# A second place in PSUM for the logarithm from the ninth unit on, two places for x instead of three

## The chip, the cores and the metric

The kernel runs on one core of one Trainium2 chip. The core has five engines that work side by side and meet only at semaphores: PE (TensorE, matmuls), DVE (VectorE), ACT (ScalarE), POOL (GpSimd) and SP (SyncE, which here issues all transfers). The metric is the time of one execution on the device, in microseconds (us), lower is better; a median of several runs is given.

## What is computed

Four layers one after another on x of shape (2, 96, 48, 48), each `x = x + layer(group_norm(x))`. The change lies in the first layer, in the part that makes the step sizes of a selective scan (four scan directions k, 192 channels, L = 2304 positions, two images):

```python
dlt, b, c = (dbc[:, :, :R], dbc[:, :, R:R + N], dbc[:, :, R + N:])
dlt = jnp.einsum('bkrl,kdr->bkdl', dlt, dt_proj_w) + dt_proj_b[None, :, :, None]
dlt = jax.nn.softplus(dlt)
dA = dlt[..., None] * A_log[None, :, :, None, :]
phi = jnp.exp(-jnp.cumsum(dA, axis=3))
dbx = dlt[..., None] * jnp.swapaxes(b, 2, 3)[:, :, None] * xs[..., None]
h = phi * jnp.cumsum(dbx / (phi + 1e-12), axis=3)
y = jnp.einsum('bkdln,bknl->bkdl', h, c) + Ds[None, :, :, None]
```

Softplus is computed as max(x, 0) + log(1 + exp(-|x|)), and the sum of the logarithm is corrected and capped: with e = exp(-|x|) the kernel forms max(x, 0) + e + min(log(1 + e) - e, 0).

## The kernel before

`program` runs the stages in a row, and a barrier stands between them: `group_norm`, `l0_project`, `l0_steps`, `l0_scan` and so on. The change is in `l0_steps`, which lies between 119 and 288 us of the span; `l0_scan` follows and takes about half of the program.

`l0_steps` works on U = 36 units: 12 pairs of a row tile (3 tiles of 128 rows = channel and image) and a direction (4), each cut in 3 segments of SEG = 768 positions. For each unit i these steps follow one another:

- PE, L431: x = the up-projection, two matmuls (512 and 256 columns, fp32) into a place of two PSUM banks, `base(i)`.
- ACT, L488: e = |x|, then L497: e = exp(-e), in one of NE = 3 buffers.
- DVE, L538: dl = max(x, 0) + e, in one of ND = 4 buffers. It reads x from PSUM and is the last reader of x; its semaphore `s_s` frees the place of x.
- u = -(1 + e), for even units on ACT (L493), for odd units on DVE (L543), in one of NW = 2 buffers.
- ACT, L505: the logarithm log(-u), written to PSUM.
- DVE, L547: ln = (u + 1) + ln, in place in PSUM; then L551: dl = min(ln, 0) + dl, which is the last reader of the logarithm and raises `s_dl`.
- SP, L383: dl is stored to DRAM. POOL, L585: v = XI (or its turned copy XT) times dl, which SP stores too (L387).

PSUM has 8 banks. Before the change x has two places (banks 0-1, 2-3) up to unit 7, and three from unit 8 on (banks 6-7 as well, once the chunks of b and c that used them have been evacuated). The logarithm has one place, banks 4-5, for all units. So x of unit i waits until L538 of unit i-3 has read (i-2 in the first units), and L505 of a unit waits until L551 of the unit before has read (`act.wait_ge(s_dl, i - 1)`).

The order on each engine is written out by hand as a loop over i, and each loop runs one unit ahead of its last steps. ACT in turn i: L488 of unit i, L493 of unit i-1 (if i-1 is even), L497 of unit i, L505 of unit i-1. DVE in turn i: L538 of unit i, L543 of unit i (if odd), L547 and L551 of unit i-1. PE: x of unit i. ACT also evacuates the chunks of b and c (L462, in turns 1 to 6) and casts them to bf16 parts (L472, L479). POOL computes the remainders of these parts (L559, L566, 128x2304 each) and makes the turned copy XT (L571) at units 0, 14 and 26. SP stores all this in an order of its own: behind dl of unit 6 and of unit 11 it issues four large stores (`c_rows`), and behind others the parts (`part_rows`).

Of the kernel before, what the change touches and what calls it, by code (L numbers as in the profile page):

```python
# [18 lines left out]
ACT = mybir.ActivationFunctionType  # L19
# [9 lines left out]
NC = L // CH  # L29
BANK = 512  # L30
SEG = 2 * CH
# [274 lines left out]
def l0_steps(nc, a, ps, XI, Z, d, w_bc, w_dt, w_up, al):  # L306
# [6 lines left out]
    with ExitStack() as ctx:  # L313
        sb, sem = space(nc, ctx, "l0s")
        NE, NW, ND = 3, 2, 4
# [8 lines left out]
        e, u = sb("e", [128, NE, SEG]), sb("u", [128, NW, SEG])  # L324
# [3 lines left out]
        s_x, s_ab, s_e, s_ln, s_u, s_uv, s_q, s_s, s_dl, s_vv = map(sem, "x ab e ln u uv q s dl vv".split())  # L328
# [3 lines left out]
        s_part = [sem(f"part{i}") for i in range(3)]  # L332
        block = ctx.enter_context(nc.Block())

        SLOT3 = 8

        def slot(i):

            return i % 2 if i < SLOT3 else (i - SLOT3 + 2) % 3

        def base(i):
            return (0, 2, 6)[slot(i)] * BANK

        def before(i):

            return max((j for j in range(i) if slot(j) == slot(i)), default=None)

        def place(i):
            g = i // UN
# [1 line left out]

        def by_vector(i):
            return i % 2 == 1

        LN = 4 * BANK

        @block.sync
        def _(sp):
# [42 lines left out]
        @block.tensor  # L401
        def _(pe):
            for c in range(NC):
                for t in range(T):
                    mm = pe.matmul(ps[:, c * BANK:c * BANK + CH], w_dt[:, t, :], XI[:, t, c * CH:(c + 1) * CH],
                                   start=(t == 0), stop=(t == T - 1))
                mm.then_inc(s_dt, 1)

            def bc_chunk(q):
                m, c = divmod(q, NC)  # L410
                if q >= 2:
                    pe.wait_ge(s_bce, q - 1)
                o = (6 + q % 2) * BANK
                for t in range(T):
                    mm = pe.matmul(ps[:, o:o + CH], w_bc[:, m, t, :], XI[:, t, c * CH:(c + 1) * CH],
                                   start=(t == 0), stop=(t == T - 1))
                mm.then_inc(s_bc, 1)

            def x_unit(i):
                g, _, _, c0 = place(i)  # L420
                if before(i) is None:
                    if slot(i) < 2:
                        pe.wait_ge(s_pa, NC)
                        pe.wait_ge(s_pd, NC)
                    else:
                        pe.wait_ge(s_bce, 2 * NC)
                else:
                    pe.wait_ge(s_s, before(i) + 1)
                o = base(i)
                for lo, hi in ((0, BANK), (BANK, SEG)):  # L430
                    mm = pe.matmul(ps[:, o + lo:o + hi], w_up[:, g, :], P[:, c0 + lo:c0 + hi], start=True, stop=True)  # L431
                mm.then_inc(s_x, 1)

            bc_chunk(0)
            bc_chunk(1)
            x_unit(0)
            x_unit(1)
            for i in range(2, U):
                x_unit(i)
                for q in range(2 * (i - 1), 2 * i):  # L440
                    if q < 2 * NC:
                        bc_chunk(q)

        @block.scalar
        def _(act):
            act.preload_act_table_set("natural_log_exp_and_others")
            act.wait_ge(s_in, 16)
            act.wait_ge(s_one, 1)
            for c in range(NC):
                act.wait_ge(s_dt, c + 1)  # L450
                for k in range(2):
                    rows = slice(32 * k, 32 * k + 32)
                    ins = act.activation(scan_order(P, k)[rows, 8 * c:8 * c + 8, :],
                                         ps[rows, c * BANK:c * BANK + CH].rearrange("p (h w) -> p h w", w=W),
                                         ACT.Identity, bias=one[rows, :])
                ins.then_inc(s_pa, 1)

            def evacuate(q):
                m, c = divmod(q, NC)
                act.wait_ge(s_bc, q + 1)  # L460
                for r in range(2):
                    ins = act.copy(scan_order(bc[:, m, :], 2 * m + r)[64 * r:64 * r + 64, 8 * c:8 * c + 8, :],  # L462
                                   ps[64 * r:64 * r + 64, (6 + q % 2) * BANK:(6 + q % 2) * BANK + CH]
                                   .rearrange("p (h w) -> p h w", w=W))
                ins.then_inc(s_bce, 1)

            def cast_hi(m):
                act.wait_ge(s_bce, NC * (m + 1))
                if m:
                    act.wait_ge(s_part[0], 16 * 4)  # L470
                    act.wait_ge(s_rest, 1)
                act.copy(parts[:, 0, :], bc[:, m, :]).then_inc(s_hi, 1)  # L472

            def cast_mid(m):
                act.wait_ge(s_rest, m + 1)
                if m:
                    act.wait_ge(s_part[1], 16 * 4)
                    act.wait_ge(s_lo, 1)
                act.copy(parts[:, 1, :], rest[:, :]).then_inc(s_mid, 1)  # L479

            for i in range(U + 1):
                if i < U:
                    act.wait_ge(s_x, i + 1)
                    if i >= NE:
                        act.wait_ge(s_s, i - NE + 1)
                        if by_vector(i - NE):
                            act.wait_ge(s_uv, (i - NE) // 2 + 1)
                    act.activation(e[:, i % NE, :], ps[:, base(i):base(i) + SEG], ACT.Abs).then_inc(s_ab, 1)  # L488
                if i and not by_vector(i - 1):
                    act.wait_ge(s_e, i)  # L490
                    if i > NW:
                        act.wait_ge(s_q, i - NW)
                    act.activation(u[:, (i - 1) % NW, :], e[:, (i - 1) % NE, :], ACT.Identity, bias=neg_col[:, :],  # L493
                                   scale=-1.0).then_inc(s_u, 1)
                if i < U:
                    act.wait_ge(s_ab, i + 1)
                    act.activation(e[:, i % NE, :], e[:, i % NE, :], ACT.Exp, scale=-1.0).then_inc(s_e, 1)  # L497
                if i:
                    if by_vector(i - 1):
                        act.wait_ge(s_uv, (i - 1) // 2 + 1)  # L500
                    else:
                        act.wait_ge(s_u, (i - 1) // 2 + 1)
                    if i >= 2:
                        act.wait_ge(s_dl, i - 1)
                    act.activation(ps[:, LN:LN + SEG], u[:, (i - 1) % NW, :], ACT.Ln, scale=-1.0).then_inc(s_ln, 1)  # L505
                if i == 0:
                    act.mul(na[:, :, 0:N], al[:, :, :], -1.0).then_inc(s_na, 1)
                    act.mul(na[:, :, N:2 * N], al[:, :, :], -0.5).then_inc(s_na, 1)
                for q in range(2 * (i - 1), 2 * i):
                    if 0 <= q < 2 * NC:  # L510
                        evacuate(q)
                for m in range(2):
                    if i == 3 + 5 * m:
                        cast_hi(m)
                    if i == 6 + 5 * m:
                        cast_mid(m)

        @block.vector
        def _(dve):
            dve.memset(neg_col[:, :], -1.0).then_inc(s_one, 1)  # L520
            dve.wait_ge(s_in, 16)
            for c in range(NC):
# [4 lines left out]
                                            ps[rows, c * BANK:c * BANK + CH].rearrange("p (h w) -> p h w", w=W),  # L527
                                            one[rows, :], None, ALU.add)
                ins.then_inc(s_pd, 1)
            ln = ps[:, LN:LN + SEG]  # L530

            for i in range(U + 1):
                if i < U:
                    dve.wait_ge(s_e, i + 1)
                    if i >= ND:
                        dve.wait_ge(s_vv, i - ND + 1)
                        dve.wait_ge(s_dst[i % ND], 16 * (i // ND))
                    dve.scalar_tensor_tensor(dl[:, i % ND, :], ps[:, base(i):base(i) + SEG], 0.0, e[:, i % NE, :],  # L538
                                             ALU.max, ALU.add).then_inc(s_s, 1)
                    if by_vector(i):  # L540
                        if i >= NW:
                            dve.wait_ge(s_q, i - NW + 1)
                        dve.tensor_scalar(u[:, i % NW, :], e[:, i % NE, :], -1.0, -1.0, ALU.mult, ALU.add  # L543
                                          ).then_inc(s_uv, 1)
                if i:
                    dve.wait_ge(s_ln, i)
                    dve.scalar_tensor_tensor(ln, u[:, (i - 1) % NW, :], 1.0, ln, ALU.add, ALU.add).then_inc(s_q, 1)  # L547
                    dve.wait_ge(s_q, i)
                    dve.wait_ge(s_s, i)
                    ds = dl[:, (i - 1) % ND, :]  # L550
                    dve.scalar_tensor_tensor(ds, ln, 0.0, ds, ALU.min, ALU.add).then_inc(s_dl, 1)  # L551
# [1917 lines left out]
```

## Time and profile before

| | |
|---|---|
| median of 3 runs | 3032.25 us (3024.64 to 3033.62) |
| profiled execution | 3024.85 us, span 3023.0 us |
| granted TensorE clock, mean over the span | 0.921 |
| DVE busy | 2569.6 us (85%) |
| PE, ACT, POOL busy | 2205.4, 1569.5, 1983.6 us |
| the stretch 119 to 292 us: DVE, ACT, POOL, PE busy | 124.67, 120.84, 91.85, 89.83 us of 173 |
| the same stretch: granted clock | 0.81 |
| steps of one unit on DVE: L538, L547, L551 | 0.95, 0.96, 0.96 us each |
| steps of one unit on ACT: L488, L497, L505, L493 | 0.80, 0.84, 0.81, 0.92 us each |

How to read it: the first three lines are times of whole executions. The profile is of one execution, and its rows give start and length of instructions in us from the start of the span. Busy time of an engine is the sum over its instructions; an engine can be idle because it waits for another one, and the profile names that one as the releaser. The granted clock is a share of TensorE's full 2.4 GHz.

### The profile page before, as it was taken

How to read it: one execution, taken by the hardware profiler on the slowest of the kernel's cores; microseconds unless marked ns; L12 is line 12 of the kernel's file. 1: busy time of each engine (PE TensorE's matmuls, PEld its weight loads, DVE VectorE, ACT ScalarE, POOL GpSimd, SP SyncE). 2: the span in 40 equal slices, each digit the busy share in tenths (PEclk: the TensorE clock that was granted, in tenths of full speed). 3: DMA queues.
4: the chain of work that ended last, by engine and by line, in shares of the span. 5: the costliest groups of instructions: out<-in, count | busy, mean ns of one | idle time of the engine just before them, and what ended most of it. 6: DMA issues, size and time to landing. Idle time of an engine off the chain costs nothing. (4 is left out here: it accounts for less than half of the span.)

```text
span 3023.0 us, 25175 instructions
## 1 busy us (share of the span) xinstructions
PE 2205.4 (73%) x7478; PEld 1083.3 (36%) x7478; DVE 2569.6 (85%) x2153; ACT 1569.5 (52%) x2283; POOL 1983.6 (66%) x1119
## 2 busy tenths in 40 slices
PE   6853666767776767777767677778986999688479
PEld 3421223333333333333333333333432555344344
DVE  5677999999999999999999999965887776789630
ACT  2565677677676767767767677743230000362220
POOL 0164999999999999999999999973000000297000
PEclk9977899999999999999999999997997999899689
DMA  1286334333343333334334343343005543100360
GB/s 47 86 240 231 99 104 119 103 121 115 104 123 104 117 114 109 119 102 123 112 110 118 104 118 104 118 142 95 0 0 153 127 112 79 38 8 8 85 86 24
DMA packets 144682, 303.92 MB, mean 101 GB/s; under 512 B 53725, under 2 KB 69220, under 8 KB 139556
## 3 DMA queue, kind: packets, MB, share of 16 engines
q1 hardware_dynamic: 143460, 298.19, 34.2%
q10 hardware_dynamic: 1088, 4.13, 0.6%
q8 instruction: 62, 1.02, 0.1%
q14 instruction: 72, 0.59, 0.1%
HBM read 215.46 MB, written 46.87 MB: 87 GB/s over the span
## 5 line engine op out<-in xcount | busy, mean ns | idle before, releaser
L834 POOL TENSOR_TENSOR l0c_r<-l0c_r,l0c_v 128x768 f32<-128x768 f32 x576 | 1049.2, 1843 | 25.1 <-DVE l0c_r L797 24.4
L864 ACT ACTIVATE ps<-l0c_dlt,l0c_na 128x512 f32<-128x512 f32 (+1 forms) x1152 | 625.9, 575 | 516.6 <-DVE l0c_h L823 502.7
L843 POOL TENSOR_TENSOR l0c_hcp<-l0c_cb,l0c_h 128x768 f32<-128x768 f32 x384 | 707.9, 1844 | 1.5 <-DVE l0c_h L823 1.5
L823 DVE TENSOR_TENSOR_SCAN l0c_h<-ps,l0c_h,l0c_r 128x768 f32<-128x768 f32 x384 | 693.1, 1805 | 1.2 <-issue 1.2
L755 PE MATMUL ps<-l0c_hcp,net_ident 128*128 128x512 f32 (+1 forms) x1536 | 593.4, 511 | 14.0 <-ACT l_Z L857 7.2
L874 ACT ACTIVATE l0c_r<-l0c_S,l0c_floor,l0c_na 128x768 f32<-128x768 f32 x576 | 579.7, 1013 | 0.0
L722 PE MATMUL ps<-l0c_Bp,l0c_sel 96*128 96x512 bf16 (+1 forms) x1152 | 296.7, 340 | 383.5 <-DVE l0c_hcv L804 225.0
L797 DVE SCALAR_TENSOR_TENSOR l0c_r<-l0c_r,ps 128x768 f32<-128x768 f32 x576 | 533.7, 927 | 12.8 <-PE ps L722 7.0
L755 PEld LDWEIGHTS ps<-l0c_hcp,net_ident 128*128 128x128 f32 x1536 | 274.1, 199 | 267.3 <-issue 204.6
L823 DVE TENSOR_TENSOR_SCAN l0c_h<-ps,l0c_r 128x768 f32<-128x768 f32 x192 | 335.2, 1746 | 1.0
L1429 PE MATMUL ps<-l_prod,l_wa 128*96 128x384 f32 (+1 forms) x888 | 292.3, 493 | 26.4 <-DVE l_prod L1390 26.4
L755 PE MATMUL ps<-l0c_hcv,net_ident 128*128 128x512 f32 (+1 forms) x768 | 294.5, 507 | 4.7 <-ACT l_Z L857 2.4
L722 PEld LDWEIGHTS ps<-l0c_Bp,l0c_sel 96*128 96x128 bf16 x1152 | 89.1, 99 | 569.2 <-DVE l0c_r L797 473.6
L1513 POOL MEMSET l2g_pad<- 96x224 f32 x4 | 1.1, 282 | 340.9 <-POOLq L118 340.9
L1429 PEld LDWEIGHTS ps<-l_prod,l_wa 128*96 128x96 f32 (+1 forms) x888 | 146.4, 165 | 171.8 <-issue 161.8
L172 ACT ACTIVATE net_rstd<-gn_t 96x2 f32<-96x2 f32 x4 | 0.8, 203 | 387.1 <-DVE gn_t L143 387.1
L722 PE MATMUL ps<-l0c_Cp,l0c_sel 96*128 96x256 bf16 (+1 forms) x384 | 97.8, 337 | 135.7 <-DVE l0c_r L797 134.6
L755 PEld LDWEIGHTS ps<-l0c_hcv,net_ident 128*128 128x128 f32 x768 | 136.8, 199 | 131.3 <-issue 102.4
L804 DVE TENSOR_TENSOR l0c_hcv<-ps,l0c_h 128x768 f32<-128x768 f32 x192 | 181.9, 948 | 0.0
L1628 PE MATMUL ps<-l_rows,l_diag 128*128 128x384 f32 x450 | 153.3, 503 | 35.6 <-ACT l_diag L1534 19.2
L1390 DVE TENSOR_TENSOR l_prod<-l_turned,l_other 128x2304 f32<-128x2304 f32 (+1 forms) x48 | 122.6, 2557 | 47.4 <-PE ps L1429 46.2
L1522 POOL TENSOR_TENSOR l_accp<-l_accp,l_prod 128x1152 f32<-128x1152 f32 x54 | 142.3, 2637 | 29.7 <-ACT l_prod L1547 22.0
(273 smaller groups left out, 2446.8 us busy)
## 6 DMA issues: line engine op xcount, KB each, us to landing
l0c_cb<-cf SPq DMA_DIRECT2D x768, 192.0 KB, 3.4
l_other<-l_p SPq DMA_DIRECT2D x22, 864.0 KB, 5.8
dlt<-l0s_dl SPq DMA_DIRECT2D x36, 384.0 KB, 2.3
v<-l0s_vv SPq DMA_DIRECT2D x36, 384.0 KB, 2.9
l0c_dlt<-dlt SPq DMA_DIRECT2D x36, 384.0 KB, 3.9
l0c_v<-v SPq DMA_DIRECT2D x36, 384.0 KB, 4.5
l_other<-l_p SPq DMA_DIRECT2D x22, 288.0 KB, 6.7
l0c_Bp<-bc SPq DMA_DIRECT2D x36, 144.0 KB, 4.1
```

The lines of the kernel that those rows point to most:

```text
L722: mm = pe.matmul(ps[:, lo:hi], sel[:, t % 2, n * 128:(n + 1) * 128], rows[:, i, lo - at:hi - at], start=True, stop=True)
L755: mm = pe.matmul(ps[:, lo:hi], ident[:, :], hc[:, lo - PY:hi - PY], start=(n == 0), stop=(n == N - 1))
L797: dve.scalar_tensor_tensor(rj, rj, 1.0, b_all, ALU.add, ALU.mult).then_inc(s_ub, 1)
L804: dve.tensor_tensor(hcv[:, dve_steps(j) % NHV, :], c_all, h[:, j % N, :], ALU.mult).then_inc(s_hv, 1)
L823: dve.tensor_tensor_scan(h[:, n, :], da[j % 2], r[:, j % NR, :], init, ALU.mult, ALU.add).then_inc(s_scan, 1)
L834: pool.tensor_tensor(r[:, j % NR, :], r[:, j % NR, :], v[:, (j // N) % 2, :], ALU.mult).then_inc(s_w, 1)
L843: pool.tensor_tensor(hcp[:, p % NHP, :], cb[:, p % NCB, :], h[:, e % N, :], ALU.mult).then_inc(s_hp, 1)
L864: act.activation(da[e % 2][:, part], dlt[:, i, part], ACT.Exp, scale=na[:, i, n:n + 1]).then_inc(done, 1)
L874: act.activation(r[:, j % NR, :], S[:, i, :], ACT.Tanh, bias=floor[:, :], scale=na[:, i, N + n:N + n + 1]).then_inc(s_tanh, 1)
L1429: mm = pe.matmul(ps[0:C, o:o + CH], wa[0:height, i, :], prod[0:height, n % NPR, c * CH:(c + 1) * CH], start=(i == 0), stop=(i == PT - 1))
L1522: pool.tensor_tensor(accp[:, tl, :], accp[:, tl, :], prod[:, g % NPR, :], ALU.add).then_inc(s_ptap, 1)
L1628: mm = pe.matmul(ps[:, o:o + CH], diag[:, tl, i, :], rows[:, tl, dy + 8 * c:dy + 8 * c + 8, dx:dx + W], start=(i == 0), stop=(i == NPE - 1))
```

## The change

The three places of x become two for all units (banks 0-1 and 2-3), and x of unit i waits for L538 of unit i-2 throughout. The two banks that become free (6-7) are the second place of the logarithm from unit 8 on: `log_slot` gives unit 8 the second place, unit 9 the first, and so on in turn. `before(i)` is now the last unit with the same place of the logarithm, so L505 of unit i waits for L551 of unit i-2 from unit 10 on; that of unit 8 waits until the chunks of b and c have left the banks. No instruction is added or taken away, and the order on each engine is the same; only the PSUM addresses and the waits differ.

```diff
-        SLOT3 = 8
-
-        def slot(i):
-
-            return i % 2 if i < SLOT3 else (i - SLOT3 + 2) % 3
+        SECOND = 8
 
         def base(i):
-            return (0, 2, 6)[slot(i)] * BANK
+            return (0, 2)[i % 2] * BANK
+
+        def log_slot(i):
+
+            return 0 if i < SECOND else (i - SECOND + 1) % 2
+
+        def log(i):
+            o = (4, 6)[log_slot(i)] * BANK
+            return ps[:, o:o + SEG]
 
         def before(i):
 
-            return max((j for j in range(i) if slot(j) == slot(i)), default=None)
+            return max((j for j in range(i) if log_slot(j) == log_slot(i)), default=None)
...
             def x_unit(i):
                 g, _, _, c0 = place(i)
-                if before(i) is None:
-                    if slot(i) < 2:
-                        pe.wait_ge(s_pa, NC)
-                        pe.wait_ge(s_pd, NC)
-                    else:
-                        pe.wait_ge(s_bce, 2 * NC)
+                if i < 2:
+                    pe.wait_ge(s_pa, NC)
+                    pe.wait_ge(s_pd, NC)
                 else:
-                    pe.wait_ge(s_s, before(i) + 1)
+                    pe.wait_ge(s_s, i - 1)
...
-                    if i >= 2:
-                        act.wait_ge(s_dl, i - 1)
-                    act.activation(ps[:, LN:LN + SEG], u[:, (i - 1) % NW, :], ACT.Ln, scale=-1.0).then_inc(s_ln, 1)
+                    if before(i - 1) is not None:
+                        act.wait_ge(s_dl, before(i - 1) + 1)
+                    elif log_slot(i - 1):
+                        act.wait_ge(s_bce, 2 * NC)
+                    act.activation(log(i - 1), u[:, (i - 1) % NW, :], ACT.Ln, scale=-1.0).then_inc(s_ln, 1)
...
                 if i:
+                    ln = log(i - 1)
                     dve.wait_ge(s_ln, i)
                     dve.scalar_tensor_tensor(ln, u[:, (i - 1) % NW, :], 1.0, ln, ALU.add, ALU.add).then_inc(s_q, 1)
```

## Rows read from the trace of the kernel before

**Rows 1.** Waits, 119 to 292 us: who waited for whom, total us, times, longest

```profile
ACT ps L505 <- DVE l0s_dl L551: 34.9, 15, 5.1
DVE l0s_dl L538 <- ACT l0s_e L497: 33.4, 21, 5.8
```

**Rows 2.** Windows, 226 to 254 us: busy us of each engine, clock, DMA share

```profile
226.00:254.00 28.00, 12.46 (x32) 5.42 (x32) 26.10 (x29) 21.49 (x28) 16.16 (x9) 1.00 0.58 232
```

**Rows 3.** Timeline of DVE, units 21 to 24: start us, us, line, operation

```profile
233.24 0.94 DVE L538 SCALAR_TENSOR_TENSOR l0s_dl<-ps,l0s_e 128x768 f32<-128x768 f32 x1
234.27 0.96 DVE L547 SCALAR_TENSOR_TENSOR ps<-l0s_u,ps 128x768 f32<-128x768 f32 x1
235.26 0.96 DVE L551 SCALAR_TENSOR_TENSOR l0s_dl<-ps,l0s_dl 128x768 f32<-128x768 f32 x1
236.55 0.96 DVE L538 SCALAR_TENSOR_TENSOR l0s_dl<-ps,l0s_e 128x768 f32<-128x768 f32 x1 [0.33 <-ACT l0s_e L497]
237.42 1.16 DVE L543 TENSOR_SCALAR l0s_u<-l0s_e 128x768 f32<-128x768 f32 x1
238.50 0.95 DVE L547 SCALAR_TENSOR_TENSOR ps<-l0s_u,ps 128x768 f32<-128x768 f32 x1
239.49 0.96 DVE L551 SCALAR_TENSOR_TENSOR l0s_dl<-ps,l0s_dl 128x768 f32<-128x768 f32 x1
240.36 0.95 DVE L538 SCALAR_TENSOR_TENSOR l0s_dl<-ps,l0s_e 128x768 f32<-128x768 f32 x1
```

**Rows 4.** Timeline of ACT, same pair: logarithm of unit 21, exponential of unit 23

```profile
233.42 0.81 ACT L505 ACTIVATE ps<-l0s_u 128x768 f32<-128x768 f32 x1 [1.72 <-DVE l0s_dl L551]
...
235.69 0.83 ACT L497 ACTIVATE l0s_e<-l0s_e 128x768 f32<-128x768 f32 x1
```

**Rows 5.** Timeline of DVE, unit 12

```profile
191.06 0.96 DVE L538 SCALAR_TENSOR_TENSOR l0s_dl<-ps,l0s_e 128x768 f32<-128x768 f32 x1 [2.51 <-ACT l0s_e L497]
191.93 0.95 DVE L547 SCALAR_TENSOR_TENSOR ps<-l0s_u,ps 128x768 f32<-128x768 f32 x1
```

**Rows 6.** Line 543: duration ns min/median/max, first and last start us

```profile
L543 DVE TENSOR_SCALAR l0s_u<-l0s_e x18: 548/1160/3655, 126.4 to 280.8; 128x768 f32<-128x768 f32 x18
```

**Rows 7.** Timeline of POOL, units 13, 21, and 26 to 27

```profile
204.47 2.13 POOL L585 TENSOR_TENSOR l0s_vv<-l0e_XI,l0s_dl 128x768 f32<-128x768 f32 x1
...
236.35 1.81 POOL L585 TENSOR_TENSOR l0s_vv<-l0s_XT,l0s_dl 128x768 f32<-128x768 f32 x1 [1.09 <-DVE l0s_dl L551]
...
252.29 4.53 POOL L571 COPY l0s_XT<-l0e_XI 128x2304 f32<-128x2304 f32 x1
256.67 3.61 POOL L585 TENSOR_TENSOR l0s_vv<-l0e_XI,l0s_dl 128x768 f32<-128x768 f32 x2
```

**Rows 8.** Timeline of DVE, line 543 of units 15, 27 and 29, line 547 of 28

```profile
202.20 2.73 DVE L543 TENSOR_SCALAR l0s_u<-l0s_e 128x768 f32<-128x768 f32 x1
...
251.66 1.10 DVE L543 TENSOR_SCALAR l0s_u<-l0s_e 128x768 f32<-128x768 f32 x1
...
258.72 1.98 DVE L543 TENSOR_SCALAR l0s_u<-l0s_e 128x768 f32<-128x768 f32 x1
260.62 0.95 DVE L547 SCALAR_TENSOR_TENSOR ps<-l0s_u,ps 128x768 f32<-128x768 f32 x1
```

**Rows 9.** Timeline of DVE, line 538 of unit 16

```profile
212.15 0.96 DVE L538 SCALAR_TENSOR_TENSOR l0s_dl<-ps,l0s_e 128x768 f32<-128x768 f32 x1 [5.35 <-DMA dlt<-l0s_dl]
```

**Rows 10.** Timeline, end of the stage: units 34, 35, and SP's next load

```profile
282.90 0.96 DVE L551 SCALAR_TENSOR_TENSOR l0s_dl<-ps,l0s_dl 128x768 f32<-128x768 f32 x1
...
284.80 0.96 DVE L547 SCALAR_TENSOR_TENSOR ps<-l0s_u,ps 128x768 f32<-128x768 f32 x1 [0.94 <-ACT ps L505]
...
291.83 0.34 SPq L688 DMA_DIRECT2D l0c_sel<-in_sel  x1
```

**Rows 11.** Timeline of PE, x of units 27 and 32

```profile
241.36 1.56 PE L431 MATMUL ps<-l0s_P,l0e_w_up 128*128 128x512 f32 x4 [2.25 <-DVE l0s_dl L538]
...
258.86 2.93 PE L431 MATMUL ps<-l0s_P,l0e_w_up 128*128 128x512 f32 x4 [1.72 <-DVE l0s_dl L538]
```

More of the change, by code:

```diff
@@ L353, in by_vector @@
             return i % 2 == 1
-        LN = 4 * BANK
         @block.sync
@@ L529, in _ @@
                 ins.then_inc(s_pd, 1)
-            ln = ps[:, LN:LN + SEG]
             for i in range(U + 1):
```

## The prediction

> **What bounds the kernel now.** The program is four layers in a row with barriers between the stages, so a stage that ends earlier by t starts everything behind it earlier by t. The change touches only the step sizes, from 119 to 288 us of a 3023 us span. I read the waits of that stretch first [rows 1]. The longest wait that the change can reach is ACT's: the logarithm (L505) waits 34.9 us in 15 waits, because it has one place and L551 of the unit before reads it. The next is DVE's own: L538 waits 33.4 us for the exponential (L497). But that table covers the start of the stage too, where ACT also evacuates bc. In the even part behind it DVE is busy 26.10 of 28.00 us [rows 2], and ACT's idle time costs nothing while DVE has work. So the question is how much DVE idles, and that is read off DVE's own rows.
>
> I call the steps of unit i by letters: X (PE, L431), Abs (L488), Exp (L497), Ln (L505), S (L538), U (L543 on DVE for odd units, L493 on ACT for even ones), Q (L547), D (L551), V (POOL, L585). A pair of units on DVE is S even, Q odd, D odd, S odd, U odd, Q even, D even. [Rows 3] show the pair from S of unit 22 at 233.24 to S of unit 24 at 240.36: 7.12 us. DVE stands still in it at two places only: 0.33 us before S23 (waits for Exp), and between S22 and Q21, whose starts are 1.03 us apart. There Q waits for Ln, which ends at 233.42 + 0.81 = 234.23 [rows 4]. Where Ln is long done the same two starts are 0.87 apart, 191.06 to 191.93 [rows 5]. So 0.33 + 0.16 us per pair can be had at most.
>
> **The 0.33 is not to be had, because U is tied to POOL.** U starts at 237.42 and takes 1.16 us [rows 3], though its shortest is 0.55 [rows 6]. It ends at 238.58. V on POOL runs from 236.35 to 238.16 [rows 7]: U ends 0.42 behind it. The same in a long case: U from 202.20 ends at 204.93 [rows 8], 0.4 behind POOL's instruction, which gave way to V at 204.47 [rows 7]. So U, once POOL is at work, ends 0.42 us after POOL's current instruction, however early U began. V in turn starts 0.13 us after D of the odd unit has ended (235.26 + 0.96 + 0.13 = 236.35). So from D odd (235.26) to Q even (238.50) it is 3.24 us with or without the wait before S odd: taking the 0.33 away makes U 0.33 longer.
>
> **What the change does, part by part.**
> (a) *Ln waits for D of two units before instead of one.* Ln23 waits at present until D22 ends (239.49 + 0.96 = 240.45); then it needs only U23, which ends at 238.58 [rows 3]. So it is done before S24 ends, and Q23 follows S24 by 0.87: gain 1.02 or 1.03 less 0.87, 0.155 us per pair. Pairs that follow one another freely are those whose S even is unit 18, 20 ... 34, nine in all. That of unit 28 is counted under (c), so 8 x 0.155 = 1.24.
> (b) *Before unit 17* other waits end last and take the gains back: long instructions on POOL hold U for up to 3.66 us [rows 6], and S16 waits 5.35 us for the store of dl of unit 12 [rows 9], which stands in SP's queue behind four large stores. One 0.155 (at S10) gets through: by D9, V9, POOL's remainder, U11 and D10 it moves SP's queue from the store of unit 10 on. Bounds 0 and 0.155; I take 0.15, since SP issues without a gap from there to unit 12.
> (c) *Unit 29, beside the turned copy.* POOL runs L571 (from 252.29), then two V in a row (256.67, 3.61 us for both): the first ends at 256.67 + 1.80 = 258.47, the second at 260.28 [rows 7]. U29 starts at 258.72, after the first has ended, and is held by the second until 260.70; Q28 follows at 260.62 [rows 8]. In the changed kernel U29 comes sooner. U27 ends at 252.76 [rows 8], tied to POOL, so not moved against it. Q26 starts 0.08 before U27's end, at 252.68; then by the distances of [rows 3, 5] D26 0.99, S28 0.87, Q27 0.87, D27 0.99, S29 0.87, U29 0.87 later, together 5.46: U29 starts at 258.14, 0.33 before 258.47. It is then held by the first V only, ends at 258.47 + 0.42 = 258.89, and Q28 comes at 258.81 instead of 260.62: 1.81. This needs U to be served ahead of a POOL instruction that stands ready behind the current one. U27 shows that: started at 251.66, it ended at 252.76, though L571 had started at 252.29 and takes 4.53 [rows 7, 8]. Bounds of this term: 0.15 (U misses the gap) and 1.81; I take 1.81, since the distances repeat to 0.02 from pair to pair.
> (d) *The end.* Ln35 waits at present for D34 (starts 282.90), and Q35, which waits for Ln35, starts at 284.80, 1.90 later [rows 10]. Then nothing holds it, and Q35 follows D34 by the 0.88 at which any instruction follows D: gain 1.02.
> (e) *x has two places instead of three.* X of unit i waits for S of i-2 instead of i-3. The ring is: S(i-2) ends, X, Abs, U of the even unit on ACT, Exp, S(i). X takes 1.56 us, or 2.93 at the slower clock [rows 11]. On ACT it is 236.52 - 234.23 = 2.29 us from the end of Ln to the end of Exp [rows 4], which is Abs, U and Exp. With 0.05 for each of three hand-overs the ring takes at most 5.4 us; from the end of S to S two units on there are 6.96 - 0.96 = 6.0. So it costs nothing even at the slow clock, and S odd may slip by another 1.1 us before U would start after V's end. Bounds: nothing, and 4.2 us lost, the whole gain.
> (f) No engine's order of instructions changes. X8 and X9, which now wait for S6 and S7, are wanted by ACT only 3 us after they can be ready. Nothing.
>
> Sum: 1.24 + 0.15 + 1.81 + 1.02 = 4.22 us. The next stage starts with SP's loads at 291.83 [rows 10] and moves as a whole. Profiled execution: 3024.85 - 4.2 = 3020.65. It stands 7.4 us below the median of the three runs (3032.25); all four executions lie near 3024.7 or 3033. Against the median the forecast is 3032.25 - 4.2 = **3028.0 us**.
>
> **Two rules from the notes.** For U's hold the 0.42 us behind POOL's end stands. The Trainium skill, SBUF — State Buffer, section on who interferes with whom, says that VectorE and GpSimd share a pair of ports as an exclusive lock for a whole instruction, and that the loser "fully blocks"; by that, and the trace agrees, removing S's wait gains nothing, while shares of a port would give the second rival below. It does not tell which of two waiting instructions comes next, on which (c) rests. For PE the rows show X at 1.56 and 2.93 us. The Trainium skill, TensorE: Matmul & The Clock Gate, Part 1, says that the clock is halved where PE has lately been little busy, which speaks against waiting longer with X; with every X slow the sum would still be 4.2, by the 5.4 above.
>
> **The rivals.**
> - *U29 misses the gap.* 4.2 - 1.66 = 2.5 us gained: 3029.7. For it: only 0.33 us of room. Chance 0.14.
> - *U and POOL share instead of excluding each other*, so that U ends earlier when it starts earlier: nine times 0.33 more, 4.2 + 3.0 = 7.2: 3025.0. Against it: U ends 0.4 behind POOL whether it began 0.7 us before that or 2.3. Chance 0.04.
> - *The ring of x takes the place of the wait*: PE, ACT and DVE turn in step, and the 0.155 per pair and (c) are lost; 0 to 1 us gained (the end's 1.02), 3032. It decides where X takes over 3.5 us. Chance 0.10.
> - *POOL is served first*: if U27, now earlier by 0.33, lost to L571, U27 would end at about 252.3 + 4.1 + 0.4 = 256.8 instead of 252.76: 4.1 lost and (c) with it, 4.2 - 1.8 - 4.1 = 1.7 us slower than before: 3034.0. It decides where L571 starts (252.29), and there U27 would have stood ready for 1.0 us instead of 0.6, which speaks for U. Chance 0.04.
> - *The change does not do what it says*, because Ln still waits for something that ends as late as D: 3032.2. Against it: U23 ends 1.9 us before D22. Chance 0.04.
>
> **How the numbers follow.** Forecast 0.58, rivals 0.36, and 0.06 for something later in the program that answers to the shift. All these cases lie within 9 us, no more than the fastest and slowest of the runs shown (3024.64 and 3033.62), so those set the range: the lower level 3024.6 - 4.2 = 3020.4, with the shared port 3017.5; the upper 3033.6, with the slow rival 3035.3. So 3018 to 3035. A measurement here can tell 0.3% (9.1 us) from no change. No case of the change reaches that alone; only the two levels of the runs can: faster 0.07, same 0.89, slower 0.04.
>
> **What would show it.** In the profile after: L505's waits for L551 gone from unit 18 on; S even to Q odd 0.87 apart; pairs of 6.97 us; U some 1.5 us long instead of 1.16, still ending 0.42 behind V; U29 of about 0.75 us; no wait of Q35 for Ln; SP's first load of the next stage at about 287.6. I am wrong if U's end moves against V's, if S odd still waits for Exp, or if X comes later than ACT is free.

## The result, and the profile after

The changed kernel takes 3022.82 us (median of 19 runs, 3016.34 to 3026.02); the kernel before, measured beside it, 3027.11 us (median of 19 runs, 3024.16 to 3033.62). The ratio is 0.9982, 95% interval 0.9975 to 0.9989: a gain of 5.4 us, between 3.3 and 7.6. That is a real gain and below the 0.3% from which I had called a change faster. The profiled execution after took 3025.32 us (span 3023.5 us), no less than that of before (3024.85, span 3023.0); what is known of the reason stands under "The changed kernel again".

Here is the timeline of DVE in the changed kernel, for the pair that [rows 3] show before (start us, us, line, operation; L537 is the old L538, L542 the old L543):

```profile
232.58 0.94 DVE L537 SCALAR_TENSOR_TENSOR l0s_dl<-ps,l0s_e 128x768 f32<-128x768 f32 x1
233.45 0.95 DVE L547 SCALAR_TENSOR_TENSOR ps<-l0s_u,ps 128x768 f32<-128x768 f32 x1
234.43 0.96 DVE L551 SCALAR_TENSOR_TENSOR l0s_dl<-ps,l0s_dl 128x768 f32<-128x768 f32 x1
235.31 0.95 DVE L537 SCALAR_TENSOR_TENSOR l0s_dl<-ps,l0s_e 128x768 f32<-128x768 f32 x1
236.17 1.58 DVE L542 TENSOR_SCALAR l0s_u<-l0s_e 128x768 f32<-128x768 f32 x1
237.68 0.95 DVE L547 SCALAR_TENSOR_TENSOR ps<-l0s_u,ps 128x768 f32<-128x768 f32 x1
238.66 0.96 DVE L551 SCALAR_TENSOR_TENSOR l0s_dl<-ps,l0s_dl 128x768 f32<-128x768 f32 x1
239.53 0.95 DVE L537 SCALAR_TENSOR_TENSOR l0s_dl<-ps,l0s_e 128x768 f32<-128x768 f32 x1
```

And POOL and ACT beside it, from their own timelines:

```profile
235.52 1.81 POOL L585 TENSOR_TENSOR l0s_vv<-l0s_XT,l0s_dl 128x768 f32<-128x768 f32 x1 [0.91 <-DVE l0s_dl L551]
```

```profile
233.83 0.80 ACT L506 ACTIVATE ps<-l0s_u 128x768 f32<-128x768 f32 x1
235.18 0.81 ACT L487 ACTIVATE l0s_e<-ps 128x768 f32<-128x768 f32 x1 [0.54 <-PE ps L430]
236.02 0.84 ACT L496 ACTIVATE l0s_e<-l0s_e 128x768 f32<-128x768 f32 x1
237.79 0.81 ACT L506 ACTIVATE ps<-l0s_u 128x768 f32<-128x768 f32 x1 [0.93 <-DVE l0s_u L542]
```

Both of DVE's gaps are gone: no wait before the second L537, and L547 follows L537 by 0.87 us instead of 1.03. The logarithm no longer waits for L551, only for U (L542). But U has grown from 1.16 to 1.58 us. It ends at 237.75, and V on POOL ends at 235.52 + 1.81 = 237.33: 0.42 behind it, as before. From L551 (234.43) to L547 (237.68) it is 3.25 us, where it was 3.24. So the pair takes 6.95 us instead of 7.12, a gain of 0.16 or 0.17, and the removed wait of 0.33 sits inside U.

The pair at unit 29, where [rows 7, 8] show U held until the second V was through. DVE, then POOL:

```profile
256.97 0.82 DVE L542 TENSOR_SCALAR l0s_u<-l0s_e 128x768 f32<-128x768 f32 x1
257.71 0.95 DVE L547 SCALAR_TENSOR_TENSOR ps<-l0s_u,ps 128x768 f32<-128x768 f32 x1
```

```profile
251.13 4.55 POOL L571 COPY l0s_XT<-l0e_XI 128x2304 f32<-128x2304 f32 x1
255.56 3.90 POOL L585 TENSOR_TENSOR l0s_vv<-l0e_XI,l0s_dl 128x768 f32<-128x768 f32 x2
```

The second V alone:

```profile
257.33 2.13 POOL L585 TENSOR_TENSOR l0s_vv<-l0e_XI,l0s_dl 128x768 f32<-128x768 f32 x1
```

U took 0.82 us instead of 1.98 and ended at 257.79, some 0.4 after the first V. The second V, started at 257.33, took 2.13 instead of 1.81, so it was V that waited. And the end of the stage, which [rows 10] show before:

```profile
279.48 0.96 DVE L551 SCALAR_TENSOR_TENSOR l0s_dl<-ps,l0s_dl 128x768 f32<-128x768 f32 x1
280.36 0.95 DVE L547 SCALAR_TENSOR_TENSOR ps<-l0s_u,ps 128x768 f32<-128x768 f32 x1
```

```profile
287.50 0.34 SPq L688 DMA_DIRECT2D l0c_sel<-in_sel  x1
```

The next stage starts at 287.50 instead of 291.83, 4.33 us earlier.

### The profile page after: what moved, and what is told of

Same layout as the page of the kernel before. It is cut to its first block and busy times, and to the rows that moved or that the text cites. A ratio compares the mean times of both kernels' runs of the same rounds, so it can differ in the third digit from the quotient of the medians.

```text
span 3023.5 us, 25175 instructions
## 1 busy us (share of the span) xinstructions
PE 2196.0 (73%) x7478; PEld 1078.5 (36%) x7478; DVE 2569.3 (85%) x2153; ACT 1569.9 (52%) x2283; POOL 1983.1 (66%) x1119
## 3 DMA queue, kind: packets, MB, share of 16 engines
q8 instruction: 62, 1.02, 0.1%
## 5 line engine op out<-in xcount | busy, mean ns | idle before, releaser
L843 POOL TENSOR_TENSOR l0c_hcp<-l0c_cb,l0c_h 128x768 f32<-128x768 f32 x384 | 699.1, 1821 | 0.7 <-DVE l0c_h L823 0.6
```

The costliest lines, as they stand in the source:

```text
L843: pool.tensor_tensor(hcp[:, p % NHP, :], cb[:, p % NCB, :], h[:, e % N, :], ALU.mult).then_inc(s_hp, 1)
```

## The experiments

For all of them I give the time from the start of S of unit 0 to the start of D of unit 35 ("whole stage"), and from the start of S of unit 18 ("from unit 18"), behind DVE's last wait for a store (only in v_and_rows DVE waits for one once more, 0.77 us at unit 20). Both are differences of two starts in one profile. "Pair" is the length that most pairs from unit 18 on have; that of unit 28, beside the turned copy, differs (7.94 before, 6.19 after), and so do a few others in v_after_u, v_and_rows and x_three. The kernels second28, second27, x_twice, x_three and again were run once each (3027.71, 3025.53, 3028.92, 3047.49 and 3023.07 us), so only their profiles are read.

| kernel | whole stage | from unit 18 | pair |
|---|---|---|---|
| before | 163.04 | 66.74 | 7.12 |
| after | 158.73 | 62.60 | 6.95 |
| x2_log1 | 162.88 | 66.75 | 7.12 |
| second28 | 161.38 | 65.01 | 7.12, at the end 6.95 |
| second27 | 160.45 | 63.48 | 7.12, at the end 6.95 |
| v_after_u_one_log | 156.88 | 60.64 | 6.51 |
| v_after_u | 151.42 | 55.38 | 5.93 |
| x_twice | 161.36 | 62.72 | 6.95 |
| x_three | 180.58 | 73.14 | 7.74 |
| v_and_rows | 158.06 | 59.28 | 5.93 |
| again | 158.78 | 62.61 | 6.95 |

### x with two places, the logarithm with one (x2_log1)

```diff
-        SECOND = 8
+        SECOND = U
```

> One part of the change alone: x has two places for all units, the logarithm keeps its one place (SECOND = 36). Measure: from the start of S of unit 0 to the start of D of unit 35, 163.04 us in the profile before and 158.73 in the profile after. Theory (U tied to POOL, the ring of x has room): x costs nothing, 163.0, within 0.2; DVE's pairs stay at 7.12 us. Rival (the ring of x takes part of the gain): 0.2 to 0.4 us more per pair, 165 to 167.

162.88 us, and 66.75 from unit 18 on where before has 66.74. Against before the ratio is 0.9999 (0.9989 to 1.0008). The third place of x was worth nothing, so its loss costs nothing, and all of the gain is the logarithm's.

### The second place from unit 28, and from unit 27 (second28, second27)

```diff
-        SECOND = 8
+        SECOND = 28
```

> The second place of the logarithm from unit 28 on instead of unit 8, x with two places. Ln of unit 27 still waits for D of unit 26, so S of unit 29 still waits 0.33 and U of unit 29 starts after the first of the two V has ended. Theory: three S-to-Q gains of 0.155 (units 30, 32, 34) and 1.02 at the end, 163.04 - 1.49 = 161.55 from S of unit 0 to D of unit 35; U of unit 29 is 1.98 us long. Rival (U simply gets shorter or longer with DVE's own order, POOL has no part): as with the second place from 27 on, within 0.2.

> The second place of the logarithm from unit 27 on, one unit earlier than in the run with 28. Now Ln of unit 27 waits for nothing of DVE but U, S of unit 29 is not held, and U of unit 29 starts about 0.23 us before the first V ends. Theory (U waits for POOL's current instruction only): U of unit 29 takes about 0.65 us instead of 1.98, and the stage is 1.81 shorter than with 28: 159.74. Rival (no lock, or POOL's next instruction comes first): 0.16 to 0.5 us shorter than with 28, 161.1 to 161.4.

These two differ by one unit in a number, and their U of unit 29 does not start at the same point against V. In second28 (DVE, then POOL):

```profile
256.41 0.96 DVE L537 SCALAR_TENSOR_TENSOR l0s_dl<-ps,l0s_e 128x768 f32<-128x768 f32 x1 [0.33 <-ACT l0s_e L496]
257.29 1.95 DVE L542 TENSOR_SCALAR l0s_u<-l0s_e 128x768 f32<-128x768 f32 x1
```

```profile
255.23 3.58 POOL L585 TENSOR_TENSOR l0s_vv<-l0e_XI,l0s_dl 128x768 f32<-128x768 f32 x2
```

In second27:

```profile
257.77 0.95 DVE L537 SCALAR_TENSOR_TENSOR l0s_dl<-ps,l0s_e 128x768 f32<-128x768 f32 x1
258.64 0.84 DVE L542 TENSOR_SCALAR l0s_u<-l0s_e 128x768 f32<-128x768 f32 x1
```

```profile
257.25 3.91 POOL L585 TENSOR_TENSOR l0s_vv<-l0e_XI,l0s_dl 128x768 f32<-128x768 f32 x2
```

U starts 2.06 us after the first V in the one and 1.39 after it in the other. A V takes 1.8, so the one falls into the second V and takes 1.95, the other into the first and takes 0.84. (I had expected 0.65 for it, from a start 0.23 us before the first V ends; it was 0.41.) From unit 18 on, 65.01 against 63.48. The forecast was 66.74 - 1.49 = 65.25 and 1.81 less, 63.44. The 0.24 by which second28 is shorter than forecast is for the most part its pair of unit 18, which took 6.90 instead of 7.06: L537 of unit 18 had waited 0.44 us for a store, and Ln was done by then. Over the whole stage, on which I had put my expectation (159.74 for second27), the two differ by only 0.93 instead of 1.81. Up to S of unit 16, which waits for a store, second27 took 90.06 us and second28 88.94; the part from unit 18 on is the one that tells.

### V after U, with both places and with one (v_after_u, v_after_u_one_log)

One more wait on POOL, in the changed kernel and in the kernel before:

```diff
                 pool.wait_ge(s_dl, i + 1)
+                if i % 2 and 17 <= i < U - 2:
+                    pool.wait_ge(s_uv, (i + 3) // 2)
```

> The changed kernel with one more wait on POOL: V of an odd unit i from 17 on waits until U of unit i+2 is done, so that DVE's U never stands behind V. Theory (U is tied to V by the shared ports): U of units 19 and on takes 0.55 us instead of 1.5 to 1.58, D odd to Q even falls from 3.24 to 2.23, a pair from 6.95 to 5.96; nine pairs, less the 1.66 already had at unit 29 and up to 1 lost around the turned copy: 151.2 (150 to 153) instead of 158.73 from S of unit 0 to D of unit 35, and the whole time 7 to 8 us less than after. Rival (ACT or the ring of x bounds the pair as well): no more than 0.3 per pair, 156 or more; if V comes too late for the stores, it is slower than after.

> The kernel before (one place for the logarithm, three for x) with the wait of V of odd units from 17 on for U of unit i+2. Theory (two causes in series: POOL's hold of U covers ACT's wait; once the hold is gone, the logarithm's one place bounds): U of 0.55 us, but S odd still waits for Exp, which follows Ln, which waits for D: from D even to the next S odd but one it stays at 4.17 us, then 0.87 + 0.47 + 0.98, so pairs of 6.49 us instead of 7.12; from S of unit 0 to D of unit 35 157 (155.5 to 158.5) against 163.04 before and 151.4 with both. So the second place would be worth 0.5 per pair where U is free, and 0.155 where it is not. Rival (the second place is worth the same either way): pairs of 6.1, 154.

DVE in v_after_u:

```profile
229.54 0.96 DVE L551 SCALAR_TENSOR_TENSOR l0s_dl<-ps,l0s_dl 128x768 f32<-128x768 f32 x1
230.41 0.95 DVE L537 SCALAR_TENSOR_TENSOR l0s_dl<-ps,l0s_e 128x768 f32<-128x768 f32 x1
231.28 0.95 DVE L547 SCALAR_TENSOR_TENSOR ps<-l0s_u,ps 128x768 f32<-128x768 f32 x1
232.27 0.96 DVE L551 SCALAR_TENSOR_TENSOR l0s_dl<-ps,l0s_dl 128x768 f32<-128x768 f32 x1
233.14 0.95 DVE L537 SCALAR_TENSOR_TENSOR l0s_dl<-ps,l0s_e 128x768 f32<-128x768 f32 x1
234.01 0.55 DVE L542 TENSOR_SCALAR l0s_u<-l0s_e 128x768 f32<-128x768 f32 x1
234.47 0.96 DVE L547 SCALAR_TENSOR_TENSOR ps<-l0s_u,ps 128x768 f32<-128x768 f32 x1
```

From L551 at 232.27 to L547 at 234.47 it is 2.20 us instead of 3.24, and U takes 0.55. POOL waits now instead:

```profile
234.79 1.81 POOL L587 TENSOR_TENSOR l0s_vv<-l0s_XT,l0s_dl 128x768 f32<-128x768 f32 x1 [2.32 <-DVE l0s_u L542]
```

The pair is 5.93 us, the stage 151.42 (forecast 151.2). Two pairs are longer: that of unit 28 takes 6.53, since U of unit 29 still stands behind the turned copy (1.17 us), and that of unit 32 takes 6.37. Timed, v_after_u is at 0.9967 of before (0.9955 to 0.9980), 10.0 us, where after is at 0.9982. That is the lowest ratio of this study, and 4.6 us below after. I had expected 7 to 8; the two intervals are too wide to tell these apart. With one place for the logarithm U is as short, but S odd waits for Exp again (v_after_u_one_log):

```profile
234.63 0.96 DVE L538 SCALAR_TENSOR_TENSOR l0s_dl<-ps,l0s_e 128x768 f32<-128x768 f32 x1 [0.33 <-ACT l0s_e L497]
235.50 0.55 DVE L543 TENSOR_SCALAR l0s_u<-l0s_e 128x768 f32<-128x768 f32 x1
235.97 0.96 DVE L547 SCALAR_TENSOR_TENSOR ps<-l0s_u,ps 128x768 f32<-128x768 f32 x1
```

Pairs of 6.51 (forecast 6.49), stage 156.88 (forecast 157), ratio 0.9984 (0.9975 to 0.9993). So the second place of the logarithm is worth 0.17 per pair as long as POOL holds U, and 6.51 - 5.93 = 0.58 once it does not. The two costs lie over one another.

### x computed twice and three times (x_twice, x_three)

```diff
-                for lo, hi in ((0, BANK), (BANK, SEG)):
+                for lo, hi in ((0, BANK), (BANK, SEG)) * 2:
```

> The changed kernel with the two matmuls of x issued twice into the same place, so X takes about 3.1 us at the full clock. Theory (ring of x at most 5.6 of the 6.0 us there are; PE delays X odd by some 0.4 more, and S odd may slip by 1.1 before U is late): 158.7 to 159.2 from S of unit 0 to D of unit 35, as after (158.73); perhaps a wait of S odd for Exp of 0.1 to 0.4 that U swallows. Rival (x is in the ring already): 0.5 to 1.5 us more per pair, 165 or more.

> The changed kernel with the matmuls of x issued three times: X takes about 4.7 us at the full clock. Theory: two X need 9.4 us of PE per pair of 6.95, so PE bounds each pair, at about 9.5 us, in step with S; from S of unit 16 on 9 pairs x 2.5 us more, and much of the units before: 185 or more from S of unit 0 to D of unit 35. This shows what the ring costs when it does decide. Rival: none in earnest; it gives the scale for the run with two.

In x_three the factor is 3. PE in x_twice, two x in a row in 5.57 us, then in x_three (the row begins at the edge of the view):

```profile
230.94 5.57 PE L430 MATMUL ps<-l0s_P,l0e_w_up 128*128 128x512 f32 x16 [0.82 <-DVE l0s_dl L537]
237.90 5.57 PE L430 MATMUL ps<-l0s_P,l0e_w_up 128*128 128x512 f32 x16 [1.38 <-DVE l0s_dl L537]
```

```profile
225.66 20.68 PE L430 MATMUL ps<-l0s_P,l0e_w_up 128*128 128x512 f32 x56
```

With x twice, from unit 18 on the stage takes 62.72 us against 62.60: the ring of x has the room that was claimed. My expectation for the whole stage (158.7 to 159.2) was missed, with 161.36: 2.4 us are lost before unit 16, 1.8 of them by unit 3, where PE has the chunks of b and c to do as well; I had not counted them. With x three times PE does not pause from 224.65 to 274.29 us, and the pair is 7.74 us (180.58 for the stage, where I had expected 185 or more). I had expected pairs of 9.5, from 4.7 us for a tripled x, and that was wrong: one x alone takes 1.56 us for its four matmuls, 0.39 each, while matmuls in a row come every 20.68 / 56 = 0.37 us at mixed clocks and 5.57 / 16 = 0.35 in x_twice. A pair has 24 of them, 7.74 / 24 = 0.32 each. There it is PE's own work that fills the pair, so x_three does not show what the wait for one of two places costs. Up to 5.6 us of PE time per pair the two places cost nothing from unit 18 on; the kernel has about 3.

### The large stores one by one (v_and_rows)

v_after_u, with the stores of the rows of c spread over four units each:

```diff
-            def c_rows(m):
+            def c_rows(m, which):
...
-                for r in range(4):
+                for r in which:
...
-                    if i == 6 + 5 * m:
-                        c_rows(m)
+                    if 0 <= i - 6 - 5 * m < 4:
+                        c_rows(m, [i - 6 - 5 * m])
```

> The changed kernel with V of odd units from 17 on after U of unit i+2, and the four large stores of the rows of c given one per unit (after dl of units 6 to 9 and 11 to 14) instead of four at once. Theory (S of units 11 and 16 wait for stores of dl that stand behind four large stores in SP's queue): these waits, 3.1 and 4.9 us with V moved alone, shrink to 0 to 2 us each, and the stage is 3 to 6 us shorter than with V moved alone: 146 to 148.5 instead of 151.42 from S of unit 0 to D of unit 35. Rival (the transfers themselves are the limit, the queue order is not): the waits move to other units and the stage stays within 1.5 us of 151.4.

Of the waits the rival was right: they moved. L537 of unit 11 no longer waits for a store (2.81 us in v_after_u), but that of unit 12 then waits 7.26 us for Exp instead of 2.89 and starts only 0.1 us earlier. L537 of unit 16 waits 0.72 us instead of 4.9, but those of units 17 and 18 wait 3.57 and 4.25, and that of unit 19 waits 2.96 for Exp:

```profile
207.69 0.96 DVE L537 SCALAR_TENSOR_TENSOR l0s_dl<-ps,l0s_e 128x768 f32<-128x768 f32 x1 [0.72 <-DMA dlt<-l0s_dl]
...
214.07 0.96 DVE L537 SCALAR_TENSOR_TENSOR l0s_dl<-ps,l0s_e 128x768 f32<-128x768 f32 x1 [3.57 <-DMA dlt<-l0s_dl]
...
221.62 0.96 DVE L537 SCALAR_TENSOR_TENSOR l0s_dl<-ps,l0s_e 128x768 f32<-128x768 f32 x1 [4.25 <-DMA dlt<-l0s_dl]
```

The stage is 158.06 us, 6.6 longer than v_after_u, and the ratio to before 0.9984 (0.9975 to 0.9993). So both numbers were missed, the theory's and the rival's 1.5 us. The waits moved and grew. The order in SP's queue does matter, by 6.6 us here, but spreading the large stores loses time; why the waits grew, and whether another order would gain, no run shows.

### The changed kernel again (again)

> The changed kernel once more, unaltered, for one more profile. In the profile after, the stage ends 4.3 us earlier but the span is 0.5 us longer than before: 3.5 us of that come between the end of the scan and the first channel-mixing stage, 1985 to 2130 us. Theory (that part differs from one execution to the next): the stage is again 158.7 from S of unit 0 to D of unit 35, within 0.3, while the time from the start of the next stage to the end of the program is not that of the profile after, but 1 to 5 us away from it. Rival (the shift by 4.3 us is given back there by the change itself): the time behind the stage repeats within 0.5 us.

The stage repeated: 158.78 us. The part behind it did not settle the question as I had put it: it was 2.5 us shorter than in the profile after, yet about as much was lost again before the channel mixing. Its first matmul (L1100) starts at 2100.94 us in before, at 2100.08 in after and at 2100.46 in again, so that of the 4.33 and 4.09 us by which the next stage's first load came earlier only 0.86 and 0.48 are left. Most of what is lost is PE's clock. Here is PE in before and in after, at the start of the same 36 matmuls (L974):

```profile
2056.71 11.77 PE L974 MATMUL ps<-l0n_sq,l0n_avgv 128*2 128x384 f32 x36 [2.89 <-ACT l0n_sq L990]
```

```profile
2052.90 14.71 PE L974 MATMUL ps<-l0n_sq,l0n_avgv 128*2 128x384 f32 x36 [2.89 <-ACT l0n_sq L990]
```

Both follow a pause of PE of 2.89 us. The windows of before and after there (window, us, busy us of PE, PEld, DVE, ACT, POOL, granted clock, DMA share, GB/s):

```profile
2056.90:2059.90 3.00, 3.00 (x10) 0.76 (x9) 0.55 (x1) 0.00 (x0) 2.60 (x3) 1.00 0.79 211
```

```profile
2053.10:2056.10 3.00, 3.00 (x6) 0.56 (x5) 0.00 (x0) 0.00 (x0) 2.46 (x3) 0.50 0.77 232
```

In before the clock stays at 2.4 GHz (1.00); in after it is 1.2 GHz (0.50) for about 6 us, and the matmuls take 2.9 us longer (14.71 against 11.77). Of the eleven profiles of this study, three show the loss there (after, again, second28, each with 14.71 us) and eight do not (11.77 each), v_after_u, second27 and v_after_u_one_log among them, whose stages are shortened too. So neither a shorter stage nor the second place of the logarithm is enough to bring it about. But the changed kernel shows it in both its profiles, and the kernel before was profiled once. If the loss belonged to the changed kernel, 4.3 - 2.9 = 1.4 us would be left of the gain, and the interval of the timed gain (3.3 to 7.6 us) speaks against that. What puts an execution on one side or the other stays open.

The clock is not all of it. From the next stage's first load to the end of the span it is 2731.2 us in before, the shortest of all eleven profiles; the other seven without the loss have 2732.8 to 2735.2, the three with it 2733.5 to 2737.0. So two single profiles cannot show a gain of 4 us in the whole program; the stage alone can, and the timed runs.

## Why the prediction was right, and where it was not

**U is tied to POOL.** Right. The 0.33 us before S odd went into U, which ends 0.42 us behind V at both starts, and moving V away instead brings 1.04 us between D odd and Q even. The Trainium skill, SBUF — State Buffer, section on who interferes with whom, has the two engines exclude each other on a shared pair of ports; the trace agrees, with a U of 0.55 us alone and up to 3.65 behind POOL.

**(a) S to Q.** Predicted 0.155 per pair, measured 0.16, in all nine pairs.

**(b) Before unit 17.** Predicted 0.15; from S of unit 0 to S of unit 16 it was 89.39 before and 89.22 after, 0.17. The store of unit 12 still ends last there, with a wait of 5.16 us instead of 5.35, and the four large stores ahead of it were issued 0.23 us earlier, counted from S of unit 0, as the term wanted. But x2_log1, which has no second place for the logarithm, took 89.22 as well, second28 88.94 and second27 90.06. So a term of this size cannot be told from the spread of the transfers, and that its number came out is no evidence for it.

**(c) Unit 29.** Predicted 1.81; between D of unit 26 (1.16 us earlier than before) and Q of unit 28 (2.91 earlier) 1.75 us were won. U started 0.4 us before the first V ended (0.33 predicted). That U goes ahead of a POOL instruction that stands ready was inferred from one row. The second V of 2.13 us shows it in after, and second28 against second27 shows that it hangs on the start of U. The rival in which POOL is served first is out.

**(d) The end.** Predicted 1.02; D of unit 34 is 3.42 us earlier, Q of unit 35 is 4.44: 1.02.

**(e) The ring of x.** No cost, as predicted, and x2_log1 shows it by itself. But one of my signs of being wrong did come true: in the even units from 20 on x arrives after ACT is free, by 0.54 us in most of them (0.15 to 1.91). It costs nothing, because S has more room than that: Exp of unit 24 ends at 236.02 + 0.84 = 236.86, and S of unit 24 starts at 239.53. In the odd units, for which the ring was added up, ACT does not wait for x. The sign should have been S waiting for Exp.

**The sum.** 4.22 predicted, 163.04 - 158.73 = 4.31 measured in the stage; the next stage's first load was forecast at 287.6 and came at 287.50. The gain of the whole, 5.4 us (3.3 to 7.6), takes in both. In term (b), 0.17 of the 4.31 us, the agreement may be luck; the other parts are seen each in its own rows.

**The absolute time** was the weak step: 3028.0 forecast, 3022.8 measured, inside the range by its width. I added the gain to a median of three runs, 3032.25, and 19 runs put that median at 3027.11. This is 5.1 of the 5.2 us. My reading that executions lie near 3024.7 or near 3033 came from four of them; the 19 runs fill the space between. A gain of 4 us should have been given as a ratio, with the level left wide.

## What to carry to other kernels

Before crediting a removed wait, look at the instruction behind it: if that one's length differs from case to case (0.55 to 3.65 us for the same shape), it is waiting inside itself, and the time before it will move into it. Find what its end is tied to, and move that; here one wait on POOL brought more in the stage than a second buffer did (6.2 against 4.3 us, though the timed gains of the two cannot be told apart), and made the buffer worth three times as much per pair. Where two costs cover each other, test each with the other gone.

## What the runs showed of the hardware

- DVE's TENSOR_SCALAR from SBUF to SBUF (128x768, fp32) takes 0.55 us alone. Started while a POOL instruction ran, it ended 0.41 to 0.43 us after that one in all eleven profiles, whether it had started 0.2 or 3.5 us before its end. The profile shows this hold as length of the instruction (up to 3.87 us, in x_three) and not as idle time. DVE's other steps, which read one operand from PSUM, keep their 0.94 to 0.96 us beside POOL, also inside the long turned copy.
- At the end of a POOL instruction, a DVE instruction of this kind that has been waiting went ahead of POOL's next one in each such case here, and POOL's then shows the wait (2.13 us instead of 1.81). Coming 0.4 us before that end or 0.2 after it decides over 1.1 us.
- After a pause of 2.89 us PE's clock was at 2.4 GHz in eight profiles and at 1.2 GHz in three, for the same code at the same place; 2.9 us hang on it. The Trainium skill, TensorE: Matmul & The Clock Gate, Part 1, has the gate depend on how busy PE has been recently and calls it variable from run to run; the traces agree as far as both outcomes follow the same pause, but the one kernel that was profiled twice came out alike both times.
